# First attention's queries and keys from split inputs, two tiles at a time, and context rows doubled

## The chip, the cores and the metric

The kernel runs on one core of a Trainium2 chip. The metric is the device time of one execution in microseconds (us). The engines of the core are named as in the profile: PE (TensorE, matrix products and transposes), DVE (VectorE), ACT (ScalarE), POOL (GpSimd) and SP, which issues DMAs. Each engine works through its own list of instructions in a fixed order and waits on semaphores.

## What is computed

Two cross-attention blocks follow each other on the same 16 batches. Cut to what matters, with x of 16 x 128 x 256, a context of 16 x 128 x 192 and 16 heads of 16 columns:

```
# block 0
xn, yn = layernorm(x, ln1), layernorm(ctx, ln2)
q = xn @ Wq;  k, v = split(yn @ Wkv)
x = x + softmax(q k^T * 16**-0.5) v @ Wproj + bproj
x = x + gelu(layernorm(x, ln3) @ W1 + b1) @ W2 + b2
# block 1
q = (x * rsqrt(mean(x*x) + 1e-5) * norm_w) @ wq
k, v = split(ctx @ wkv)
q, k = unit(rotate(q)), unit(rotate(k))
x = x + softmax(q k^T * 4) v @ wout
```

## The kernel before

One tile is one batch (128 rows). Three stages run over the 16 tiles, and overlap: the first attention (functions ending in `_a`, with `inputs_a`, `queries_keys_a`, `scores_a`), the MLP over pairs of tiles (`_b`), and the second attention (`_c`). There is no scheduler at run time: every engine's order is written out as a list of calls such as `scores_a(3)`, for PE, DVE, ACT and POOL each, and semaphores hold an engine where a value isn't ready.

A product of two float32 matrices is done in one of two ways. Either `mm` gets float32 operands (the first attention's projections, lines 1068, 1072, 1082 and 1147), or both operands are split into a high and a low part, stored as fp32r, and three matmuls are summed: high by high, high by low, low by high (`HI_LO`, `split_mm`, line 1046, and the MLP, lines 1166 and 1178). The high part is a copy on ACT, the low part is a subtraction on DVE that reads the same data again.

A tile of the first attention goes so. DVE takes statistics, centres and scales x and the context (`statistics`, `centre`, `scale`, lines 2114 to 2140). PE turns both (`inputs_a`), ACT copies the result to SBUF (`inputs_T`, line 547). PE projects queries and keys into `bank_qk` and values into `bank_o`. ACT and DVE split queries and keys (lines 553 and 2146); ACT and POOL multiply them by two masks (lines 559 and 354). PE computes the scores into the four banks `banks_s` (line 1091), DVE reduces them to row maxima (`maxima`, line 2153), splits these (`maxima_split`, 2162 and 2164), PE turns them; then PE computes the same scores again with the maxima taken off (`shifted_a`, 1091 and 1115), ACT takes the exponential (line 575), PE weights the values (1126), turns the result back (`back_a`), DVE divides (`heads_a`, 2170 and 2173), PE turns it (`normed_a`) and projects it (`project_a`, 1147), and DVE adds it to x (`residual_a`, 2179). So every tile needs DVE and PE in turn, and `banks_s` is written twice a tile.

The MLP of a pair begins with `turn_b` on PE, `lnT_b` on ACT and `split_lnT` on DVE (line 2098), behind which the first product `up_b(p, 0)` stands on PE.

`busy(n, bank)` (line 1252) puts n transposes of the identity into a bank that nobody reads. They compute nothing and stand in PE's order in front of waits; there are 98 of them, 35 in front of `up_b(1, 0)`.

## Time and profile before

| what | value |
|---|---|
| median of the runs | 365.31 us (364.48 to 365.33, three runs) |
| the profiled execution, own time | 364.97 us |
| its span, first to last instruction | 363.2 us |
| PE busy | 355.1 us, 98% of the span |
| DVE busy | 278.7 us, 77% |
| ACT busy | 252.7 us, 70% |
| POOL busy | 193.5 us, 53% |
| TensorE's granted clock | 1.00 in every slice |
| DMA share of 16 engines | 0.6, 0.9, 0.6 and 0.4 in the first four fortieths, 0.1 or less after |

PE is busy nearly all the time. DVE's share is an average: it is higher while the first attention runs than later, and the same holds, the other way round, for ACT.

### The profile page before, as it was taken

The numbers are of one execution on the slowest core, as the hardware profiler recorded it, in microseconds if no ns is written. First come the engines' busy times: TensorE is split into PE (matmuls) and PEld (weight loads), VectorE is DVE, ScalarE is ACT, GpSimd is POOL, SyncE is SP. The second block draws the span as 40 slices with busy tenths as digits, with TensorE's granted clock in tenths as the row PEclk, the third lists the DMA queues.
The fourth block names the chain that finished last, engine by engine and source line by source line (L and its number), as shares of the span: only waits on it lengthen the run. The fifth ranks groups of instructions, "written<-read, shape, count | busy, mean of one in ns | idle before, by whom it ended". The sixth has DMA issues, their size and how long they took to land.

```text
span 363.2 us, 11396 instructions
## 1 busy us (share of the span) xinstructions
PE 355.1 (98%) x4492; PEld 322.1 (89%) x4492; DVE 278.7 (77%) x654; ACT 252.7 (70%) x490; POOL 193.5 (53%) x194
## 2 busy tenths in 40 slices
PE   8999999999999998999999999999999999999996
PEld 5988888898788887899999999999999999998885
DVE  3998899868698677767876687787877777868742
ACT  2467766675676674855568988976978679966662
POOL 2357433545735247304687359449465756477920
PEclk9999999999999999999999999999999999999999
DMA  6964110000000000000000000000100000000001
GB/s 181 220 197 130 31 49 28 28 27 27 4 3 2 24 2 2 13 2 14 1 13 13 13 2 7 19 27 11 63 14 13 10 33 27 16 28 16 17 16 43
DMA packets 15724, 12.55 MB, mean 35 GB/s; under 512 B 3252, under 2 KB 15032, under 8 KB 15672
## 3 DMA queue, kind: packets, MB, share of 16 engines
q1 hardware_dynamic: 15664, 11.83, 11.3%
q8 instruction: 36, 0.59, 0.7%
q14 instruction: 16, 0.13, 0.1%
q10 hardware_dynamic: 8, 0.00, 0.0%
HBM read 9.73 MB, written 2.10 MB: 33 GB/s over the span
## 4 chain that ended last, share of the span: by engine, by line
PE 86%; DVE 6%; SPq 3%; issue 2%; DMA 1%; ACT 1%; DVEq 0%; ACTq 0%
PE banks_s L1166 12%; PE bank_qk L1046 10%; PE banks_s L1091 7%; PE bank_o L1178 7%; PE bank_y L1178 6%; PE bank_y L1230 4%; PE banks_s L1219 4%; PE bank_t L1126 4%; PE bank_y L1147 3%; PE bank_t L1046 3%; PE bank_qk L1068 3%; PE bank_o L1082 3%; PE bank_qk L1072 3%; DVE row_max L2153 3%; PE bank_o L1210 2%
## 5 line engine op out<-in xcount | busy, mean ns | idle before, releaser
L400 POOL TENSOR_TENSOR norm_inv<-norm_sq_min,minus_half 128x32 f32<-128x32 f32 x16 | 87.6, 5478 | 47.9 <-DVE norm_sq_min L2248 47.9
L354 POOL TENSOR_TENSOR masked<-qkT_r,halves_t 128x512 fp32r<-128x512 f32 x32 | 32.6, 1040 | 58.5 <-DVE qkT_r L2146 58.5
L2153 DVE TENSOR_REDUCE row_max<-banks_s 128x8 f32<-128x1024 f32 x32 | 37.6, 1216 | 2.9 <-PE banks_s L1091 2.5
L575 ACT ACTIVATE PT<-banks_s 128x1024 f32<-128x1024 f32 x32 | 31.1, 1022 | 10.1 <-PE banks_s L1115 9.7
L1166 PE MATMUL banks_s<-lnT_hi,W_hi 128*128 128x256 f32 x120 | 35.4, 295 | 0.0
L676 ACT ACTIVATE PT<-banks_s 128x1024 f32<-128x1024 f32 x32 | 31.5, 1024 | 5.5 <-PE banks_s L1219 5.2
L1166 PE MATMUL banks_s<-lnT_hi,W_lo 128*128 128x256 f32 x120 | 33.9, 282 | 0.0
L1166 PE MATMUL banks_s<-lnT_lo,W_hi 128*128 128x256 f32 x120 | 33.9, 282 | 0.0
L1091 PE MATMUL banks_s<-masked,qkT_r 32*128 32x256 f32 x768 | 31.5, 294 | 0.9 <-DVE row_max L2153 0.7
L1091 PEld LDWEIGHTS banks_s<-masked,qkT_r 32*128 32x128 f32 x768 | 25.0, 183 | 7.5 <-issue 4.7
L619 ACT ACTIVATE W_s<-banks_s,b_cols 128x256 f32<-128x256 f32 x60 | 25.0, 471 | 6.6 <-PE bank_y L1178 4.7
L2103 DVE TENSOR_TENSOR hT_lo<-W_s,hT_hi 128x512 fp32r<-128x512 f32 x32 | 21.5, 686 | 3.5 <-ACT hT_hi L622 3.4
L1166 PEld LDWEIGHTS banks_s<-lnT_hi,W_hi 128*128 128x128 f32 x120 | 22.8, 190 | 0.6 <-issue 0.6
L1166 PEld LDWEIGHTS banks_s<-lnT_lo,W_hi 128*128 128x128 f32 x120 | 22.9, 191 | 0.0
L1166 PEld LDWEIGHTS banks_s<-lnT_hi,W_lo 128*128 128x128 f32 x120 | 22.8, 190 | 0.0
L378 POOL TENSOR_TENSOR x_all<-x_all,b_row 128x256 f32<-128x256 f32 x16 | 11.5, 741 | 19.0 <-DVE normed L2093 19.0
L559 ACT ACTIVATE masked<-qkT_r,halves_t 128x512 fp32r<-128x512 f32 x32 | 21.3, 717 | 0.2
L2263 DVE SCALAR_TENSOR_TENSOR masked<-bank_o,halves_t,masked 128x256 fp32r<-128x256 f32 x32 | 14.0, 478 | 9.6 <-ACT qkT_r L669 9.5
L622 ACT ACTIVATE hT_hi<-W_s 128x512 fp32r<-128x512 f32 x31 | 19.6, 632 | 1.0
L1178 PE MATMUL bank_o<-W_hi,hT_hi 128*128 128x256 f32 x64 | 19.0, 296 | 0.0
L1178 PE MATMUL bank_y<-W_hi,hT_hi 128*128 128x256 f32 x64 | 18.4, 287 | 0.0
L1178 PE MATMUL bank_y<-W_hi,hT_lo 128*128 128x256 f32 x64 | 18.1, 283 | 0.0
(180 smaller groups left out, 1079.9 us busy)
## 6 DMA issues: line engine op xcount, KB each, us to landing
x_all<-in_x SPq DMA_DIRECT2D x16, 128.0 KB, 2.3
W_s<-in_L_xattn_W SPq DMA_DIRECT2D x2, 1024.0 KB, 7.8
out<-x_all SPq DMA_DIRECT2D x16, 128.0 KB, 1.7
ctx_in<-in_ctx SPq DMA_DIRECT2D x16, 96.0 KB, 3.0
ctx_in<-in_ctx_T SPq DMA_DIRECT2D x16, 64.0 KB, 1.8
ctx_in<-in_ctx_T SPq DMA_DIRECT2D x16, 32.0 KB, 2.1
Wq_s<-in_L_xattn_Wq SPq DMA_DIRECT2D x1, 256.0 KB, 3.7
Wkv_s<-in_L_xattn_Wkv SPq DMA_DIRECT2D x1, 256.0 KB, 3.6
```

Of the source, the lines that this page charges most:

```text
L354: nc.gpsimd.tensor_tensor(masked[:, r, 1, :, half, :], qkT_r[:, r, 1, :, :].bitcast(fp32), ones, ALU.mult)\
L400: nc.gpsimd.tensor_tensor(norm_inv[:, j, :], norm_sq_min[:, j, :], minus_half[:, :], ALU.pow).then_inc(c_norm_inv, 1)
L559: nc.scalar.activation(masked[:, t % RING, 0, :, half, :], qkT_r[:, t % RING, 0, :, :].bitcast(fp32), ACT.Copy, scale=halves_t[:, half:hal ...
L575: nc.scalar.activation(PT[:, 2 * h:2 * h + 2, :], banks_s[:, 2 * h:2 * h + 2, :], ACT.Exp, scale=HD ** -0.5)\
L619: last = nc.scalar.activation(hT[:, m, :], bank[:, 256 * k:256 * k + 256], ACT.Gelu, bias=b1_cols[:, m:m + 1])
L676: nc.scalar.activation(PT[:, 2 * h:2 * h + 2, :], banks_s[:, 2 * h:2 * h + 2, :], ACT.Exp, scale=HD ** 0.5)\
L1046: last = mm(out, a[:, x, k, :], b[:, y, k, :], start=k == n == 0, stop=k == 1 and n == 2)
L1091: last = mm(bank_s[g][:, 2 * TOK * tile:2 * TOK * (tile + 1)], qkT_r[quad(g), r, a, rows + tile, :], masked[quad(g), r, b, columns + tile, ...
L1166: last = mm(bank[:, 256 * (m % 2):256 * (m % 2) + 256], w[:, k, 128 * m:128 * m + 128], act_T[:, k, :], start=k == n == 0, stop=k == KT - ...
L1178: last = mm(bank[:, 0:C1], h[:, m, 128 * j:128 * j + 128], w[:, m, :], start=m == n == 0, stop=m == HM - 1 and n == 2)
L2103: v.tensor_tensor(hT_lo[:, part(u), :], hT[:, part(u), :], hT_hi[:, part(u), :].bitcast(fp32), ALU.subtract).then_inc(b_hT_lo, 1)
L2153: v.tensor_reduce(row_max[:, 8 * h:8 * h + 8], banks_s[:, 2 * h:2 * h + 2, :].rearrange("p n (r k) -> p (n r) k", k=TOK), AX.X, ALU.max).t ...
```

## The change

Five things are changed in the code, and the orders of all engines are written anew.

- The first attention's inputs are split like those of the second: ACT writes the high part into `inT_r`, DVE subtracts the low part (`inputs_lo_a`, new). The weights Wq, Wkv and Wproj are split at the start (three copies on ACT, four subtractions on DVE, new).
- Queries and keys are projected by `queries_a(p)` and `keys_a(p)` for two tiles at once: 12 and 10 matmuls of 256 columns. Both use `bank_qk`, one after the other, so `queries_hi`, `queries_lo`, `keys_hi` and `keys_lo` are four instructions a pair, each of 128 x 512, where `queries_keys_hi` and `queries_keys_lo` were two a tile.
- The projection behind the first attention is a `split_mm` of six matmuls, with `out_lo_a` (new) on DVE.
- The context has 192 columns, 128 and 64. The last 64 are now given twice, so that the second half of the rows is full: the low part of the inputs meets them in one row range and the high part in the other. A product with the context takes five matmuls (`CTX_TERMS`) where a split one took six, in both attentions. The context's normalisation on DVE works on 256 columns where it worked on 192.
- The second attention's weights are loaded into the buffers of the first's, so three waits stand in front of their loads on SP, and `queries_weight`, `context_weight` and `out_weight` wait for the last use of the first attention's splits.

There are now 214 transposes by `busy`, 143 of them in front of `up_b(1, 0)`.

```diff
 HI_LO = ((0, 0), (0, 1), (1, 0))
+CTX_TERMS = ((0, 0, 0), (0, 1, 0), (2, 0, 0), (1, 0, 1), (3, 1, 1))
...
+            def context_mm(out, inputs, columns):
+                for n, (w, a, k) in enumerate(CTX_TERMS):
+                    last = mm(out, inputs[:, a, 2 + k, :], wkv_r[:, w, columns], start=n == 0, stop=n == 4)
+                return last
...
-            def queries_keys_a(t):
...
-                for m in range(KT):
-                    for k in range(KT):
-                        mm(bank_qk[:, 128 * m:128 * m + 128], Wq_s[:, k, 128 * m:128 * m + 128], inT[:, j, k, :],
-                           start=k == 0, stop=k == KT - 1)
...
+            def queries_a(p):
+                if p == 0:
+                    pe.wait_ge(wa_q_lo, 1)
+                pe.wait_ge(a_in_lo, 2 * p + 2)
                 for m in range(KT):
                     for k in range(KT):
+                        for n, (w, a) in enumerate(HI_LO):
+                            last = mm(bank_qk[:, 256 * m:256 * m + 256], wq_r[:, w, k, 128 * m:128 * m + 128],
+                                      inT_r[:, pair_slots(p), a, k, :], start=k == n == 0, stop=k == KT - 1 and n == 2)
+                last.then_inc(a_q_mm, 1)
...
+            def keys_a(p):
...
                 for m in range(KT):
-                    for k in range(2):
-                        last = mm(bank_qk[:, 256 + 128 * m:384 + 128 * m], Wkv_s[:, k, 128 * m:128 * m + 128],
-                                  inT[:, j, 2 + k, :], start=k == 0, stop=k == 1)
+                    for n, (w, a, k) in enumerate(CTX_TERMS):
+                        last = mm(bank_qk[:, 256 * m:256 * m + 256], wkv_r[:, w, 128 * m:128 * m + 128],
+                                  inT_r[:, pair_slots(p), a, 2 + k, :], start=n == 0, stop=n == 4)
+                last.then_inc(a_k_mm, 1)
...
             def values_a(t):
...
-                for k in range(2):
-                    last = mm(bank_o[:, 0:C1], inT[:, t % 2, 2 + k, :], Wkv_s[:, k, C1:], start=k == 0, stop=k == 1)
-                last.then_inc(A["v_mm"], 1)
+                pe.wait_ge(a_in_lo, t + 1)
+                context_mm(bank_o[:, 0:C1], inT_r[:, t % AHEAD], slice(C1, 2 * C1)).then_inc(A["v_mm"], 1)
...
             def project_a(t):
...
-                for k in range(KT):
-                    last = mm(bank_y[:, 0:C1], onT[:, k, :], Wproj_s[:, k, :], start=k == 0, stop=k == KT - 1)
-                last.then_inc(A["proj_mm"], 1)
+                pe.wait_ge(a_onT_lo, t + 1)
+                split_mm(bank_y[:, 0:C1], onT_r[:, :, :, :], wout_r[:, :, :, :]).then_inc(A["proj_mm"], 1)
...
-                split_mm(bank_t[:, C1:2 * C1], inT_r[:, t % 2, :, 2:4, :], wkv_r[:, :, :, C1:]).then_inc(C["v_mm"], 1)
+                context_mm(bank_t[:, C1:2 * C1], inT_r[:, t % 2], slice(C1, 2 * C1)).then_inc(C["v_mm"], 1)
...
-                v.scalar_tensor_tensor(yn[:, j, 0:C2], yn[:, j, 0:C2], rstd[:, j, 1:2], ln2_rows[:, 1, :],
+                v.scalar_tensor_tensor(yn[:, j, :], yn[:, j, :], rstd[:, j, 1:2], ln2_rows[:, 1, :],
                                        ALU.mult, ALU.add).then_inc(A["norm_done"], 1)
...
-            def queries_keys_lo(t):
-                r = t % RING
-                dve.wait_ge(a_qk_hi, t + 1)
-                v.tensor_tensor(qkT_r[:, r, 1, :, :], bank_qk[:, :].rearrange("p (a b) -> p a b", a=4),
-                                qkT_r[:, r, 0, :, :].bitcast(fp32), ALU.subtract).then_inc(a_qk_lo, 1)
+            def inputs_lo_a(t):
+                dve.wait_ge(A["inT_ready"], t + 1)
+                v.tensor_tensor(inT_r[:, t % AHEAD, 1, :, :], bank_t[:, :].rearrange("p (a b) -> p a b", a=4),
+                                inT_r[:, t % AHEAD, 0, :, :].bitcast(fp32), ALU.subtract).then_inc(a_in_lo, 1)
+
+            def queries_lo(p):
+                dve.wait_ge(a_q_hi, p + 1)
+                v.tensor_tensor(qkT_r[:, pair_slots(p), 1, 0:KT, :], pair_bank(bank_qk),
+                                qkT_r[:, pair_slots(p), 0, 0:KT, :].bitcast(fp32), ALU.subtract).then_inc(a_q_lo, 1)
...
+            def out_lo_a(t):
+                dve.wait_ge(A["onT_ready"], t + 1)
+                v.tensor_tensor(onT_r[:, 1, :, :], by_row(bank_y[:, 0:C1]), onT_r[:, 0, :, :].bitcast(fp32), ALU.subtract)\
+                    .then_inc(a_onT_lo, 1)
...
+            act.wait_ge(w_q_loaded, LOADED)
+            nc.scalar.activation(wq_r[:, 0], Wq_s[:, :, :], ACT.Copy).then_inc(wa_q_hi, 1)
+            act.wait_ge(w_att_loaded, LOADED)
+            nc.scalar.activation(wkv_r[:, 0:2, :], Wkv_s[:, :, :], ACT.Copy).then_inc(wa_kv_hi, 1)
             act.wait_ge(rows_spread, 1)
...
-            busy(4, bank_t)
+            busy(8, bank_t)
             inputs_a(0)
-            busy(7, bank_o)
+            busy(15, bank_o)
```

The orders are shown at three places. The first is PE at the start of the program, behind the last warming transposes. Lines 1255 (1291 after) are the fillers of `busy`, 1054 and 1056 (1085 and 1087) turn one tile's inputs, 1068 and 1072 (1097 and 1109) are queries and keys. Before:

```order
L1265 MATMUL banks_s<-ident 128x128 x8
L1255 MATMUL bank_t<-ident 128x128 x4
L1054 MATMUL bank_t<-ident,xn 128x128 x2
L1056 MATMUL bank_t<-ident,yn 128x128 x2
L1255 MATMUL bank_o<-ident 128x128 x7
L1068 MATMUL bank_qk<-inT,Wq_s 128x128 x4
L1072 MATMUL bank_qk<-inT,Wkv_s 128x128 x4
L1054 MATMUL bank_t<-ident,xn 128x128 x2
L1056 MATMUL bank_t<-ident,yn 128x128 x2
```

After:

```order
L1291 MATMUL bank_t<-ident 128x128 x8
L1085 MATMUL bank_t<-ident,xn 128x128 x2
L1087 MATMUL bank_t<-ident,yn 128x128 x2
L1291 MATMUL bank_o<-ident 128x128 x15
L1085 MATMUL bank_t<-ident,xn 128x128 x2
L1087 MATMUL bank_t<-ident,yn 128x128 x2
L1291 MATMUL bank_o<-ident 128x128 x14
L1097 MATMUL bank_qk<-inT_r,wq_r 128x256 x12
L1291 MATMUL bank_o<-ident 128x128 x15
L1109 MATMUL bank_qk<-inT_r,wkv_r 128x256 x10
L1085 MATMUL bank_t<-ident,xn 128x128 x2
```

The queries and keys of tile 0 stood behind 11 fillers and one tile's transposes; they now stand behind those of two tiles, with 37 fillers in front of the queries and 15 more in front of the keys.

The second place is DVE in the first attention: the instructions in front of a reduction to row maxima (`row_max`), that of tile 4 before and of tile 3 after. `xn` and `yn` are the normalised inputs, `on` the divided output of a tile. Before:

```order
L2162 CAST max_cols<-row_max 128x4x4
L2164 TENSOR_TENSOR max_cols<-row_max,max_cols 128x4x4
L2137 SCALAR_TENSOR_TENSOR xn<-xn,rstd,ln_rows 128x256
L2140 SCALAR_TENSOR_TENSOR yn<-yn,rstd,ln_rows 128x192
L2114 BN_STATS stats<-x_all 128x6
L2115 BN_STATS stats<-ctx_in 128x6
L2117 BN_AGGR mean_var<-stats 128x2
L2119 BN_AGGR mean_var<-stats 128x2
L2170 RECIPROCAL row_sums_inv<-bank_o 128x16
L2173 TENSOR_TENSOR on<-bank_o,row_sums_inv 128x256
L2146 TENSOR_TENSOR qkT_r<-bank_qk,qkT_r 128x512
L2153 TENSOR_REDUCE row_max<-banks_s 128x8 x2
```

After:

```order
L2206 TENSOR_TENSOR qkT_r<-bank_qk,qkT_r 128x2x256
L2193 SCALAR_TENSOR_TENSOR xn<-xn,rstd,ln_rows 128x256
L2196 SCALAR_TENSOR_TENSOR yn<-yn,rstd,ln_rows 128x256
L2243 TENSOR_TENSOR onT_r<-bank_y,onT_r 128x256
L2184 SCALAR_TENSOR_TENSOR xn<-x_all,mean_var,ln_rows 128x256
L2186 SCALAR_TENSOR_TENSOR yn<-ctx_in,mean_var,ln_rows 128x256
L2193 SCALAR_TENSOR_TENSOR xn<-xn,rstd,ln_rows 128x256
L2196 SCALAR_TENSOR_TENSOR yn<-yn,rstd,ln_rows 128x256
L2235 RECIPROCAL row_sums_inv<-bank_o 128x16
L2238 TENSOR_TENSOR on<-bank_o,row_sums_inv 128x256
L2211 TENSOR_TENSOR qkT_r<-bank_qk,qkT_r 128x2x256
L2218 TENSOR_REDUCE row_max<-banks_s 128x8 x2
```

Between two reductions there are now low parts of queries (2206), of keys (2211) and of the turned output (2243), and all rows of `yn` are 256 wide.

The third place is PE in front of the first up product of the second pair (`W_hi` by `lnT_hi` into `banks_s`, line 1166 before and 1200 after; behind `...` in the piece of before stand the rest of 24 down products of the first pair, in that of after 17 more down products and a group of 12 up products of the first pair). Before:

```order
L1133 MATMUL bank_o<-ident,oT 128x128 x4
L1046 MATMUL bank_qk<-wkv_r,inT_r 128x256 x6
L1155 MATMUL bank_t<-ident,normed 128x128 x4
L1147 MATMUL bank_y<-Wproj_s,onT 128x256 x2
L1178 MATMUL bank_o<-W_hi,hT_hi 128x256
L1178 MATMUL bank_o<-W_lo,hT_hi 128x256
...
L1178 MATMUL bank_o<-W_hi,hT_lo 128x256
L1166 MATMUL banks_s<-lnT_hi,W_hi 128x256
```

After:

```order
L1189 MATMUL bank_t<-ident,normed 128x128 x4
L1127 MATMUL banks_s<-masked,qkT_r 128x256 x24
L1151 MATMUL banks_s<-maxT,picks_wide 128x128 x16
L1139 MATMUL bank_qk<-ident,max_cols 128x128
L1175 MATMUL bank_y<-ident,on 128x128 x2
L1212 MATMUL bank_o<-W_hi,hT_hi 128x256
...
L1078 MATMUL bank_qk<-wkv_r,inT_r 128x256 x5
L1072 MATMUL bank_y<-wout_r,onT_r 128x256 x6
L1200 MATMUL banks_s<-lnT_hi,W_hi 128x256
```

Behind the transposes of the pair (`normed`) now stand the shifted scores of tile 14 (1127, 1151) and the turning of tile 15's maxima (1139). The shifted scores of tile 15, `weighted_a` and `back_a` of tiles 14 and 15, `normed_a(14)`, `project_a(14)` and six down products are behind the up product now; before, they stood in front of it.

## Rows read from the trace of the kernel before

**Rows 1.** Busy time in three stretches: span, then us and count for each engine.
```profile
20.64:160.92 140.28, 137.28 (x2118) 119.86 (x2117) 117.45 (x270) 95.54 (x168) 65.36 (x88) 1.00 0.11 33
20.64:63.85 43.21, 42.41 (x677) 37.20 (x679) 40.24 (x98) 28.70 (x49) 19.87 (x27) 1.00 0.26 80
160.92:363.20 202.28, 198.80 (x2266) 186.71 (x2264) 147.29 (x343) 148.61 (x308) 120.74 (x86) 1.00 0.06 19
```

**Rows 2.** Timeline of PE in the first attention: start us, length us, group.
```profile
70.31 1.07 PE L1126 MATMUL bank_t<-PT,vals 128*17 128x128 f32 x32
71.31 0.98 PE L1091 MATMUL banks_s<-masked,qkT_r 32*128 32x256 f32 x24
72.12 0.56 PE L1115 MATMUL banks_s<-maxT,picks_wide 32*128 32x128 f32 x16
...
73.10 1.06 PE L1068 MATMUL bank_qk<-inT,Wq_s 128*128 128x128 f32 x8
74.00 1.06 PE L1072 MATMUL bank_qk<-inT,Wkv_s 128*128 128x128 f32 x8
74.89 0.60 PE L1133 MATMUL bank_o<-ident,oT 128*128 128x128 f32 x4
...
81.37 1.03 PE L1082 MATMUL bank_o<-Wkv_s,inT 128*128 128x256 f32 x4
82.24 1.03 PE L1147 MATMUL bank_y<-Wproj_s,onT 128*128 128x256 f32 x4
```

**Rows 3.** The chain in order of time: start us, length us, engine, tile, line.
```profile
186.96 1.42 PE banks_s L1166 x12
188.38 1.43 PE bank_qk L1046 x12
```

**Rows 4.** Timeline of PE: filler transposes and the matmuls behind them.
```profile
25.41 1.25 PE L1255 MATMUL bank_y<-ident 128*128 128x128 f32 x10
26.59 0.99 PE L1091 MATMUL banks_s<-masked,qkT_r 32*128 32x256 f32 x24
```

**Rows 5.** Timeline of DVE: one of each kind of its instructions.
```profile
42.63 0.41 DVE L2179 TENSOR_TENSOR x_all<-x_all,bank_y 128x256 f32<-128x256 f32 x1
...
43.25 0.48 DVE L2137 SCALAR_TENSOR_TENSOR xn<-xn,rstd,ln_rows 128x256 f32<-128x256 f32 x1
43.65 0.41 DVE L2140 SCALAR_TENSOR_TENSOR yn<-yn,rstd,ln_rows 128x192 f32<-128x192 f32 x1
43.98 0.42 DVE L2114 BATCH_NORM_STATS2 stats<-x_all 128x6 f32<-128x256 f32 x1
...
45.51 0.26 DVE L2170 RECIPROCAL row_sums_inv<-bank_o 128x16 f32<-128x16 f32 x1 [0.64 <-PE bank_o L1133]
...
46.15 0.68 DVE L2146 TENSOR_TENSOR qkT_r<-bank_qk,qkT_r 128x512 fp32r<-128x512 f32 x1
46.74 2.34 DVE L2153 TENSOR_REDUCE row_max<-banks_s 128x8 f32<-128x1024 f32 x2
```

**Rows 6.** Timeline of POOL, ACT and PE at the start of the program.
```profile
11.91 0.60 ACT L547 ACTIVATE inT<-bank_t 128x512 f32<-128x512 f32 x1 [2.84 <-PE bank_t L1056]
16.74 2.04 POOL L354 TENSOR_TENSOR masked<-qkT_r,halves_t 128x512 fp32r<-128x512 f32 x2 [2.32 <-DVE qkT_r L2146]
18.98 0.98 PE L1091 MATMUL banks_s<-masked,qkT_r 32*128 32x256 f32 x24
```

**Rows 7.** Timeline of DVE: the first reduction, and the second pair's `lnT_lo`.
```profile
20.64 2.34 DVE L2153 TENSOR_REDUCE row_max<-banks_s 128x8 f32<-128x1024 f32 x2
...
160.24 0.68 DVE L2098 TENSOR_TENSOR lnT_lo<-bank_t,lnT_hi 128x512 fp32r<-128x512 f32 x1
```

**Rows 8.** Timeline of PE: the first up product of the second pair.
```profile
161.98 0.28 PE L1166 MATMUL banks_s<-lnT_hi,W_hi 128*128 128x256 f32 x1
```

**Rows 9.** Timeline of POOL and DVE: a mask product beside a split of maxima.
```profile
98.49 2.04 POOL L354 TENSOR_TENSOR masked<-qkT_r,halves_t 128x512 fp32r<-128x512 f32 x2 [1.69 <-DVE qkT_r L2146]
98.52 1.04 DVE L2164 TENSOR_TENSOR max_cols<-row_max,max_cols 128x16 f32<-128x16 f32 x1
```

1952 lines of the change are left out of this document (1013 added, 939 removed).

## The prediction

> **What bounds the kernel now.** I read the busy table first: PE works in 98% of the span, DVE in 77%, so the first guess is that whatever is taken off PE is gained. Then the chain of waits in order of time, which runs from one PE group straight to the next [rows 3]: it shows that PE's work, not a wait, sets the time over most of the span. Then busy time in stretches, because a share over the whole span hides which stage is near a second limit. From the first reduction of row maxima to the end of the second pair's low part, which is nearly the whole first attention, PE is busy 137.28 of 140.28 us and DVE 117.45; behind it DVE is busy 147.29 of 202.28 [rows 1]. The stretch inside it from 20.64 to 63.85 is the one to look at: PE 42.41 and DVE 40.24 of 43.21 us [rows 1]. There both engines are nearly full. So the first attention has little room on DVE, and this is where the change adds DVE work.
>
> **What PE loses and gains.** Prices are from one start to the next. Queries and keys of a tile take 0.90 + 0.89 us, its values 0.87 [rows 2], and its projection is the same two 128x256 float32 products, 0.87. A group of twelve split matmuls of 256 columns takes 1.42 [rows 3], 0.119 each. The new queries and keys are 22 of these a pair, 11 a tile, 1.31 us where 1.79 stood: 0.48 less. Values are five, 0.60: 0.27 less. The projection is six, 0.71: 0.15 less. Over 16 tiles that is 7.7 + 4.4 + 2.4. The second attention has two matmuls fewer a tile, 32 x 0.119 = 3.8. Removed: 18.2 us. Added: 116 filler transposes. Ten of them stand between 25.41 and 26.59 [rows 4], 0.118 each: 13.7 us. If nothing else moved, PE would be 4.5 us shorter: 365.0 - 4.5 = 360.5. The fillers stand in front of waits, so part of them covers waiting that would be there anyway; they can't be counted as a loss by themselves.
>
> **What DVE gains, and the sum.** I take DVE's list from the first reduction (`maxima(0)`) to `split_lnT(1)`, 117.45 us busy before [rows 1, 7], and go through what is added and what is moved out of it.
> - Twelve `inputs_lo_a`, 128x512 with one operand in PSUM, like `qkT_r` at 46.15, which gives way to the next after 0.59 [rows 5]: 0.60 each, 7.2.
> - Fourteen `out_lo_a`, 128x256 with one operand in PSUM, like the residual at 42.63, 0.33: 4.7.
> - One low part of Wproj: 0.6.
> - 22 instructions on `yn` that go from 192 to 256 columns: 0.40 for 256 (43.25 to 43.65) and 0.33 for 192 (43.65 to 43.98) [rows 5]: 22 x 0.07 = 1.5.
> - Queries' and keys' low parts are fourteen of 128x512 in either kernel: nothing. ACT has the same trade.
> - Out of the stretch go two `scale` (0.73 each), one `statistics` (0.9: 43.98 to 45.51 less the 0.64 of waiting), two `heads_a` (0.64), two `residual_a` (0.33), one `split_hT` (0.6), one memset (0.3) [rows 5]: 5.2 in all.
>
> Net 8.8, so DVE has 126.3 us to do in there.
>
> When does it begin? The first scores stood at 18.98 and the reduction at 20.64 [rows 6, 7]. Now tile 0's turned inputs are copied from 11.91 on for 0.60 [rows 6] and subtracted for 0.60; tile 1's transposes reuse the bank, so the same follows once more; twelve matmuls 1.4, copy and subtraction 1.2, ten matmuls 1.2, copy and subtraction 1.2, then POOL's masks 2.04 [rows 6]. DVE's own list in between (normalisation of four tiles, the weights' low parts at 1.2) is longer than this chain at two places: I come to 24.9 for the first scores and 26.2 for the reduction, 5.6 later than before. Half of what PE spends on fillers lies here, and it costs nothing, for the queue behind it can't start.
>
> Then the first up product of the second pair can start at 26.2 + 126.3 + 0.1 = 152.6 if DVE never idles, where it stood at 161.98 [rows 8], about 1 us behind its operand. Behind it PE had 363.2 - 162.0 = 201.2 us. Moved behind it are the shifted scores of tile 15 (0.81 + 0.5), two `weighted_a` (2.0), two `back_a` (1.0) [rows 2], `normed_a(14)`, one more projection and six down products (1.5 together); eight fillers more, 0.9; 31 context matmuls less, 3.7. Net 3.0. The sum is 152.6 + 201.2 + 3.0 = 356.8, and 1.8 outside the span (365.0 - 363.2): 358.6.
>
> What is missing is DVE's idle time in the stretch. Lower bound nothing: 358.6, which PE's own 360.5 overrules. Upper bound: the share in the stretch where both engines are nearly full, 40.24 of 43.21 [rows 1], 6.9% idle: 126.3 / 0.931 is 9.4 more, 368.0. There each engine waits for the other in turn. In the changed kernel PE has more room beside DVE than there, since its work without fillers shrinks by 0.9 us a tile while DVE's grows, so more values should lie ready when DVE comes to them; but PE's order is fixed and `banks_s` still goes back and forth twice a tile. I take half the share, 4.5 us: **363.1**. That is 1.9 below the profiled execution; the median of the runs shown is 0.3 above that execution, which I leave to the range.
>
> ACT and POOL. ACT gets four copies of weights and loses nothing; at 95.54 of 140.28 us [rows 1] it has room, except at the start, where the copies of Wq and Wkv stand in front of the rows that DVE's `centre(0)` needs. Bounds: 0, if the weights land before those rows are ready, to 2.0 for both copies (by the 0.60 of 128x512); in the range. SP now waits for the first weights' low parts in front of the second's loads, and the inputs of tile 9 on stand behind it on SP; DVE asks for them over ten calls later, so 0 to 3 us, taken as 0. The wider context rows are 128 KB a tile where 96 were: hidden after the first tiles.
>
> A rule to weigh: DVE's group at 42.63 to 46.74 shows an instruction starting about 0.08 us before the recorded end of the one in front (46.15 + 0.68 is 46.83, the next starts at 46.74) [rows 5]. The Trainium skill, VectorE: DVE Perf Modes, section The DRAIN you can't avoid, says that the next operation doesn't start until the pipe is empty. Priced by whole recorded lengths the 26 new subtractions would come to 2 us more, 365 in all; the trace does not agree that the full length is paid, and the sum goes by starts.
>
> **The rivals.**
> - PE alone sets the time, and DVE keeps up: 360.5. For it: 98% against 77%. Against it: 40.24 of 43.21 us with the smaller load.
> - DVE sets the pace of the first attention at 6.9% idle: 368.0, slower than before. Its place is the loop of scores, maxima, turned maxima and exponentials on `banks_s`, its price 9.4 us, and it decides from 6.4 us of DVE idle time on, 4.8% of the stretch (358.6 + 6.4 = 365.0). Each further hold-up adds to it: a split of maxima that meets a mask product on POOL takes 1.04 us [rows 9], so another order can move several microseconds. The Trainium skill, SBUF — State Buffer, section SBUF: two separate sides, says that a DVE operation with two SBUF inputs and a GpSimd operation hold a shared port pair for their whole length; the trace agrees, as the split at 98.52 ends at 99.56 and POOL's first of two products, 2.04 together from 98.49 on, near 99.5. Sixteen splits that each meet one would add 14 us by that rule.
> - The start goes wrong: the weights' copies on ACT hold `centre(0)` up, or the fillers are longer than the waits they cover. 2 to 3 us on top of 363.1: about 366.
>
> **Chances.** The forecast 0.42 (its own range 361 to 366), PE alone 0.22, DVE's pace 0.28, the start 0.08. A change under 0.3%, 1.1 us, can't be told from none here: faster is below 364.2, slower above 366.4. Faster: 0.22 + 0.25 of the forecast = 0.47. Within: 0.13 + 0.04 + 0.02 = 0.19. Slower: 0.04 + 0.24 + 0.06 = 0.34. The range 358.5 to 369.5 leaves one in ten on either side.
>
> **What would show it.** Right: PE's busy share falls while its idle time in the first attention grows, waits of PE on DVE's subtractions and splits appear, and DVE is busy over 93% between its first reduction and the second pair's `lnT_lo`; that product starts near 157; the first reduction is near 26; behind it PE is as full as now. Wrong: DVE idle over 6.4 us in there, a first reduction later than 28, or PE waiting on ACT or POOL. If the up product starts at 153 and PE is full, PE alone was the case.

## The result and the profile after

The changed kernel takes 368.00 us (median of ten, 365.88 to 368.45), the one before 364.91 (median of ten, 364.48 to 365.33): ratio 1.0064, 95% interval 1.0047 to 1.0082. It is 3.1 us slower; I had forecast 1.9 faster. Its ten times stand in two groups, four near 366 and six near 368; the profiled execution took 368.45, with a span of 366.3 us, so it is one of the second group.

The page of the changed kernel, busy time and the chain's shares by engine (the chain is the work that ended last, followed back from the last instruction); the last line is the same share in the kernel before:

```profile
PE 355.1 (97%) x4544; PEld 323.1 (88%) x4544; DVE 294.2 (80%) x681; ACT 259.0 (71%) x498; POOL 195.6 (53%) x194
...
PE 72%; DVE 13%; POOL 5%; issue 4%; ACT 3%; POOLq 1%; DVEq 0%; ACTq 0%
...
PE 86%; DVE 6%; SPq 3%; issue 2%; DMA 1%; ACT 1%; DVEq 0%; ACTq 0%
```

PE's busy time did not fall at all. DVE's rose by 15.5 us over the whole span, and the chain leaves PE for other engines more often.

Where the time went is seen best from two marks that both kernels have, the first and the last of DVE's sixteen pairs of reductions of row maxima. In the timeline of DVE of the changed kernel they stand here, with the second pair's `lnT_lo` (the counterparts before are in [rows 7]):

```profile
27.91 2.34 DVE L2218 TENSOR_REDUCE row_max<-banks_s 128x8 f32<-128x1024 f32 x2
...
147.26 2.35 DVE L2218 TENSOR_REDUCE row_max<-banks_s 128x8 f32<-128x1024 f32 x2 [1.39 <-PE banks_s L1127]
...
159.22 0.69 DVE L2154 TENSOR_TENSOR lnT_lo<-bank_t,lnT_hi 128x512 fp32r<-128x512 f32 x1 [0.28 <-ACT lnT_hi L614]
```

The last reduction of the kernel before, same view:

```profile
140.13 2.36 DVE L2153 TENSOR_REDUCE row_max<-banks_s 128x8 f32<-128x1024 f32 x2 [1.70 <-PE banks_s L1091]
```

So there are three parts, in us of the two profiled spans (363.2 and 366.3):

| | before | after | difference |
|---|---|---|---|
| start, to the first reduction | 20.64 | 27.91 | +7.27 |
| body, first to last reduction | 119.49 | 119.35 | -0.14 |
| behind, last reduction to the end | 223.07 | 219.04 | -4.03 |

The start loses 7.3 us, what stands behind gains 4.0, and the body, where the change was to free PE, gains nothing. Busy time in the body, before (first fence) and after, with the same columns as [rows 1]; the fourth row of the second fence is the stretch that answers to the first row of [rows 1]:

```profile
20.64:140.13 119.49, 116.56 (x1839) 101.06 (x1841) 100.55 (x228) 80.51 (x141) 59.25 (x79) 1.00 0.13 37
```

```profile
27.91:60.00 32.09, 30.45 (x476) 26.94 (x478) 31.41 (x69) 21.28 (x39) 17.08 (x23) 1.00 0.26 76
60.00:90.00 30.00, 28.95 (x492) 25.89 (x485) 28.85 (x72) 18.55 (x33) 12.74 (x19) 1.00 0.10 29
90.00:159.91 69.91, 67.55 (x1062) 60.08 (x1060) 62.96 (x138) 52.53 (x93) 35.18 (x45) 1.00 0.03 8
27.91:159.91 132.00, 126.95 (x2019) 112.90 (x2017) 123.23 (x276) 92.35 (x164) 65.00 (x85) 1.00 0.10 29
27.91:147.26 119.35, 114.71 (x1870) 101.73 (x1869) 111.59 (x250) 81.37 (x143) 63.37 (x82) 1.00 0.10 31
159.91:366.30 206.39, 202.72 (x2362) 188.66 (x2360) 150.00 (x351) 156.68 (x319) 120.73 (x86) 1.00 0.07 20
```

In the body DVE goes from 100.55 to 111.59 us and PE from 116.56 to 114.71. From 27.91 to 90 DVE works 60.3 of 62.1 us: it is full there. Its idle time stands behind that, 7.0 us between 90 and 159.91, and the longest waits in it are for PE: 2.4 us for score matmuls (the last reduction above waited 1.39) and 1.1 for projections. The second pair's up product starts 0.84 us behind the start of `lnT_lo`, 0.15 behind its end:

```profile
160.06 0.36 PE L1200 MATMUL banks_s<-lnT_hi,W_hi 128*128 128x256 f32 x1
```

It stood at 161.98 [rows 8] and I had put it at 152.6 plus 4.5, 157.1. PE's timeline in the body shows the new products, where [rows 2] had the float32 ones:

```profile
69.62 0.84 PE L1078 MATMUL bank_o<-wkv_r,inT_r 128*128 128x256 f32 x5
70.31 0.82 PE L1291 MATMUL bank_qk<-ident 128*128 128x128 f32 x6
...
78.03 0.98 PE L1072 MATMUL bank_y<-wout_r,onT_r 128*128 128x256 f32 x6
78.85 0.60 PE L1169 MATMUL bank_o<-ident,oT 128*128 128x128 f32 x4
```

From start to the next start, five matmuls of the values take 0.69 here, where I had priced 0.60, and six of the projection 0.82, where I had priced 0.71. The twelve of the queries and the ten of the keys cost more too, 1.53 and 1.29 where I had 1.42 and 1.19:

```profile
62.20 1.60 PE L1097 MATMUL bank_qk<-inT_r,wq_r 128*128 128x256 f32 x12
63.73 0.98 PE L1127 MATMUL banks_s<-masked,qkT_r 32*128 32x256 f32 x24
...
66.03 1.45 PE L1109 MATMUL bank_qk<-inT_r,wkv_r 128*128 128x256 f32 x10
67.32 0.38 PE L1175 MATMUL bank_y<-ident,on 128*128 128x128 f32 x2
```

Each group that stands between other products takes about 0.1 us more than the price from the groups of twelve of [rows 3], behind which a group of the same kind follows. And PE waits more: it is idle for 4.6 us of the body, where it was for 2.9. PE's three largest waits there, us in total, times, longest:

```profile
PE banks_s L1127 <- DVE row_max L2218: 1.8, 4, 1.0
PE bank_qk L1139 <- DVE max_cols L2229: 0.8, 1, 0.8
PE banks_s L1127 <- POOL masked L358: 0.8, 2, 0.6
```

The chain in order of time shows the same from another side. A piece of it in the changed kernel:

```profile
53.97 1.21 DVE row_max L2218
55.19 0.33 DVE x_all L2249
55.51 0.25 DVE max_cols L2227
...
55.79 0.67 DVE max_cols L2229
56.45 0.34 DVE stats L2170
56.79 0.26 DVE stats L2171
...
57.18 0.95 DVE row_max L2218
...
58.30 1.22 DVE row_max L2218
...
59.57 0.98 PE banks_s L1127 x23
```

Before, the chain ran from one PE group to the next as in [rows 3] over most of the first attention too. A piece of it:

```profile
34.78 0.39 PE banks_s L1115 x15
35.17 1.09 PE bank_qk L1068 x8
36.26 0.89 PE bank_qk L1072 x8
```

### The profile page after: what moved, and what is told of

It reads as the page before. It is cut to its first block, busy times and chain, and to the rows that moved or that the text cites. A ratio compares the mean times of both kernels' runs of the same rounds, so it can differ in the third digit from the quotient of the medians.

```text
span 366.3 us, 11549 instructions
## 1 busy us (share of the span) xinstructions
PE 355.1 (97%) x4544; PEld 323.1 (88%) x4544; DVE 294.2 (80%) x681; ACT 259.0 (71%) x498; POOL 195.6 (53%) x194
## 4 chain that ended last, share of the span: by engine, by line
PE 72%; DVE 13%; POOL 5%; issue 4%; ACT 3%; POOLq 1%; DVEq 0%; ACTq 0%
PE banks_s L1200 11%; PE bank_o L1212 7%; PE bank_y L1212 6%; PE banks_s L1127 5%; PE bank_qk L1072 5%; DVE row_max L2218 4%; PE bank_y L1266 4%; PE bank_t L1162 3%; POOL norm_inv L404 3%; PE banks_s L1255 3%; PE bank_y L1072 3%; PE bank_t L1078 2%; PE bank_qk L1097 2%; PE bank_qk L1078 2%; PE bank_qk L1109 2%
## 5 line engine op out<-in xcount | busy, mean ns | idle before, releaser
L358 POOL TENSOR_TENSOR masked<-qkT_r,halves_t 128x512 fp32r<-128x512 f32 x32 | 33.0, 1054 | 15.2 <-issue 14.1
L397 POOL TENSOR_TENSOR inT_r<-ctx_in,inT_r 128x256 fp32r<-128x256 f32 x16 | 11.8, 737 | 24.5 <-ACT inT_r L668 24.5
L339 POOL TENSOR_TENSOR var_eps<-mean_var,eps_t 128x2 f32<-128x2 f32 x16 | 4.1, 256 | 37.2 <-DVE mean_var L2175 37.2
## 6 DMA issues: line engine op xcount, KB each, us to landing
x_all<-in_x SPq DMA_DIRECT2D x16, 128.0 KB, 2.6
ctx_in<-in_ctx SPq DMA_DIRECT2D x16, 128.0 KB, 2.8
ctx_in<-in_ctx_T SPq DMA_DIRECT2D x16, 128.0 KB, 2.2
out<-x_all SPq DMA_DIRECT2D x16, 128.0 KB, 1.8
```

Source lines behind the costliest of these rows:

```text
L358: nc.gpsimd.tensor_tensor(masked[:, r, 1, :, half, :], qkT_r[:, t % AHEAD, 1, :, :].bitcast(fp32), ones, ALU.mult)\
```

## The experiments

All times are medians, and gains and losses are differences of medians. "Body" and "behind" are the parts of the table above, read off each kernel's profiled execution.

**The second attention's five matmuls, alone and taken back.** The kernel before with one matmul of six left out of the second attention's products on the context:

```
-                split_mm(bank_qk[:, C1:], inT_r[:, t % 2, :, 2:4, :], wkv_r[:, :, :, 0:C1])
+                context_mm(bank_qk[:, C1:], inT_r[:, t % 2, :, 2:4, :], wkv_r[:, :, :, 0:C1])
...
+            def context_mm(out, a, b):
+                for n, (x, y, k) in enumerate(((0, 0, 0), (0, 1, 0), (1, 0, 0), (0, 0, 1), (0, 1, 1))):
+                    last = mm(out, a[:, x, k, :], b[:, y, k, :], start=n == 0, stop=n == 4)
```

> The kernel before with one part of the change alone: the second attention's keys and values take five matmuls instead of six (the product of the low part of the last 64 context rows is left out, which doubled rows would have given). 32 matmuls of 256 columns less on PE. If PE's list sets the time to the end: 32 x 0.119 = 3.8 us gained, 361.1. If the last 37 us are set by POOL's four inverse norms (5.4 us each, in a chain with DVE), only the 26 of them ahead of the last down product count: 3.1 us gained at most, and the distance from the end of that product to the end of the kernel stays 37 us. If the saving meets waits elsewhere too: under 2 us.

Measured: 361.37 us, ratio 0.9894 (0.9872 to 0.9916), 3.65 less than the kernel before beside it (365.02). Start 20.43, body 119.56, behind 219.61 (223.07 before). The saving arrives. The distance from the last down product's last matmul to the end of the span is 37.4 us before (325.78 to 363.2) and 37.2 here (322.41 to 359.6), so nearly all of it was won ahead of it.

The same thing done whole, with the rows loaded twice and the weights laid out for it:

```
+                sp.dma_start(ctx_in[C2B:, j, TOK:2 * TOK], ctx_T[t, 128:C2, :]).then_inc(c_loaded[j], LOADED)
...
+                        v.tensor_copy(by_tile(wkv_r[0:C2B, 1, k, 0:C1]), keys[0:C2B]).then_inc(wc_lo, 1)
+                        v.tensor_tensor(by_tile(wkv_r[C2B:, 0, k, 0:C1]), keys[C2B:], by_tile(wkv_r[C2B:, 0, k, 0:C1]).bitcast(fp32),
+                                        ALU.subtract).then_inc(wc_lo, 1)
```

> The kernel before with the second attention's part of the change done whole: its context rows 128 to 191 are loaded twice, their weights are laid out as the changed kernel has them, and keys and values take five matmuls each. Nothing is left out. Against the kernel without that product (361.4) it adds one transfer of 32 KB a tile on SP and two short copies of weights on DVE. Theory PE's list: 361 to 362. Theory that the transfers or DVE's copies come in the way: above 363.

Measured: 361.40 us, ratio 0.9898 (0.9884 to 0.9912). This is the version to take: 3.6 us faster than the kernel before and 6.6 faster than the changed one.

The changed kernel with a sixth matmul back in each of these products:

```
-                context_mm(bank_qk[:, C1:], inT_r[:, t % 2], slice(0, C1))
+                context_mm(bank_qk[:, C1:], inT_r[:, t % 2], slice(0, C1), CTX_TERMS + ((2, 1, 0),))
```

> The changed kernel with a sixth matmul (low part by low part of the first 128 rows) back in each of the second attention's products on the context, 32 matmuls of 256 columns. Theory that its saving there is whole and the loss lies in the first attention's part: 3.5 to 4 us slower, 371.7. Theory that the saving is swallowed in the changed kernel (waits behind 160 us, the tail on POOL): under 2 us slower.

Measured: 371.06 us, 3.1 more than the changed kernel; start 27.84, body 119.22, behind 222.04. So the saving is there in the changed kernel as well, and without it the rest of the change, the first attention's part and the new orders together, would cost 371.06 - 364.91 = 6.2 us.

**DVE's load.** More of it in the kernel before:

```
+                wait(dve, spare_done, t)
+                v.tensor_reduce(spare[:, :], bank_qk[:, :].rearrange("p (n k) -> p n k", n=8), AX.X, ALU.max).then_inc(spare_done, 1)
                 v.tensor_tensor(qkT_r[:, r, 1, :, :], bank_qk[:, :].rearrange("p (a b) -> p a b", a=4),
```

> The kernel before with 16 more DVE instructions in the first attention: a reduction of one 128x512 bank, about 0.6 us, ahead of each tile's low part of queries and keys; its result is used by nobody. DVE gets 14 x 0.6 = 8.4 us more in the stretch from the first reduction to the second pair's low part, as much as the change adds. PE's list is untouched. DVE's busy share there would go from 84% to 90%. Theory DVE (load itself is the price): 3 to 8 us slower, 368 to 373. Theory order (the changed kernel's loss is from its start, its order and what it moves behind, not from load): under 2 us slower.

Measured: 371.89 us, ratio 1.0183 (1.0163 to 1.0203), 6.9 more. The sixteen instructions took 10.9 us, and the body grew by 6.2 for 8.9 us more of DVE's work in it:

```profile
22.05:147.72 125.67, 117.48 (x1837) 100.94 (x1841) 109.43 (x243) 80.18 (x140) 59.69 (x79) 1.00 0.11 33
```

DVE works 109.43 of 125.67 us there, 87%, and still each us of it cost over half a us. A share of busy time of 87% is no sign of room when the order is fixed. The added instruction stands right in front of the low part for which POOL's masks and the scores wait, so the run does not tell the load itself from its place; added work at a place with slack was not tried.

Less of it in the changed kernel:

```
+                n = TOK if t < AHEAD else 8
+                v.tensor_tensor(inT_r[:, t % AHEAD, 1, :, 0:n], bank_t[:, :].rearrange("p (a b) -> p a b", a=4)[:, :, 0:n],
...
+                n = TOK if t == 0 else 16
+                v.tensor_tensor(onT_r[:, 1, :, 0:n], by_row(bank_y[:, 0:C1])[:, :, 0:n], onT_r[:, 0, :, 0:n].bitcast(fp32), ALU.subtract)\
```

> The changed kernel with DVE's new subtractions cut to a small corner of each tile: inputs' low parts from tile 4 on write 8 of 128 columns a piece, the attention output's low parts from tile 1 on 16 of 128. The rest of the low parts is left over from earlier tiles, so that part of the computation is left out. PE's and all other lists are as they were. DVE has about 12 x 0.50 + 15 x 0.25 = 9.7 us less to do in the first attention. Theory DVE: 5 to 9 us gained, the kernel near 360. Theory PE: under 1.5 us gained, only at places where PE waits on DVE for a moment.

Measured: 366.67 us, 1.3 less than the changed kernel. In the body of the profiled execution, DVE's busy time falls by 6.7 us, the body by 1.4:

```profile
27.81:145.76 117.95, 114.39 (x1870) 101.68 (x1869) 104.92 (x249) 81.28 (x143) 63.53 (x82) 1.00 0.11 31
```

That is as little as the theory of PE's list allowed: DVE's load alone does not set the changed kernel's pace.

**PE's load.** Less of it in the changed kernel, then DVE and PE light together:

```
+                for n, (w, a, k) in enumerate(CTX_TERMS[0:3]):
+                    last = mm(bank_o[:, 0:C1], inT_r[:, t % AHEAD, a, 2 + k, :], wkv_r[:, w, C1:], start=n == 0, stop=n == 2)
...
+                for n, (x, y) in enumerate(HI_LO):
+                    last = mm(bank_y[:, 0:C1], onT_r[:, x, 0, :], wout_r[:, y, 0, :], start=n == 0, stop=n == 2)
```

> The changed kernel with 80 matmuls of 256 columns less on PE in the first attention: values take three of five and the projection three of six (the second half of the contraction is left out). DVE's, ACT's and POOL's lists and all fillers are as they were. PE has 80 x 0.119 = 9.5 us less. Theory PE (PE's list with its fillers sets the first attention): 6 to 9.5 us gained, about 360. Theory coupled (PE and DVE wait for each other in turn, relieving one alone gains little, as 9.7 us less on DVE gained 1.3): under 3 us gained, or a loss where the clock falls.

> The changed kernel with both loads lightened in the first attention: DVE by 9.7 us (low parts cut to a corner) and PE by 9.5 us (three matmuls for values, three for the projection). Theory PE: 1 to 2 us below the kernel with PE light alone. Theory coupled: 6 to 10 us gained against the changed kernel, several times the sum of the two single gains.

Measured: 364.95 us with PE light, 364.22 with both. The times of the first stand in groups too, six from 363.6 to 364.3 and three from 365.8 to 366.2 at the same granted clock, and its median falls between them. Group against group (365.9 and 368.1 in the changed kernel) PE light is worth 2.0 us, not the 3.05 of the medians, which is inside what the coupled theory allowed; both together are worth 3.8 by the lowest group (362.2 against 365.9) as by the medians. The two bodies:

```profile
27.36:145.26 117.90, 108.87 (x1804) 94.27 (x1804) 110.68 (x249) 80.29 (x142) 63.37 (x82) 1.00 0.10 31
```

```profile
26.98:143.19 116.21, 107.80 (x1804) 94.11 (x1804) 104.11 (x249) 80.20 (x142) 63.11 (x82) 1.00 0.10 32
```

With PE down to 107.80 and DVE to 104.11, neither is full, and the body is only 3.1 us shorter. Both single theories fall, and so does the part of the coupled one that said relieving both would give several times the sum: 3.8 against 1.3 + 2.0. What is left, by exclusion and not shown by a run of its own, is handing over between engines in an order that was written for other loads. Over this body the second largest entry of the chain by line is "issue" (time for which the profile shows no wait), 16.5%, where it was 7.1% in the changed kernel's.

PE's load less in the kernel before:

```
-                for k in range(KT):
-                    last = mm(bank_y[:, 0:C1], onT[:, k, :], Wproj_s[:, k, :], start=k == 0, stop=k == KT - 1)
+                last = mm(bank_y[:, 0:C1], onT[:, 0, :], Wproj_s[:, 0, :], start=True, stop=True)
```

> The kernel before with less for PE in the first attention: values and projection take one float32 matmul of two (half of each contraction is left out), 32 x 0.43 = 13.8 us less on PE; nothing else changes. Theory PE was the bound of the first attention before: 9 us or more gained, so that a faster product has to pay off where DVE does not take it back. Theory coupled (PE and DVE wait for each other in turn there already, as 9.6 us more on DVE cost 6.9): 3 to 7 us gained.

Measured: 360.00 us, ratio 0.9877 (0.9861 to 0.9892), 4.8 less for 13.8 us of PE work by the price from starts (PE's busy time fell by 11.2), as the coupled theory said. Body 116.01, behind 221.65. A us taken off PE in the first attention was worth 0.35 us in the kernel before, a us put on DVE in front of its low parts cost 6.9 / 10.9 = 0.63.

**The score banks.** A theory that I formed on the way: the four score banks are held in turn by scores, maxima, shifted scores and exponentials, and that ring sets the pace. Exponentials over half of their columns, in the changed kernel, in the one before, and in the changed one with PE light; and maxima over half of theirs:

```
+                n = 512 if t < 2 else 256
+                nc.scalar.activation(PT[:, 2 * h:2 * h + 2, 0:n], banks_s[:, 2 * h:2 * h + 2, 0:n], ACT.Exp, scale=HD ** -0.5)\
```

```
-                                    banks_s[:, 2 * h:2 * h + 2, :].rearrange("p n (r k) -> p (n r) k", k=TOK),
+                                    banks_s[:, 2 * h:2 * h + 2, :].rearrange("p n (r k) -> p (n r) k", k=TOK)[:, :, 0:TOK if t < 2 else TOK // 2],
```

> The changed kernel with ACT's exponentials of the first attention over half of their columns from tile 2 on (the other half is left over from earlier tiles). Each shortens the time in which the score banks are held by about 0.43 us, 0.86 a tile, 12.0 over 14 tiles; no other instruction changes, and ACT had room before (92 of 131 us). Theory loop (the four score banks, held by scores, maxima, shifted scores and exponentials in turn, some 7.0 us a tile of a period of 8.0, set the first attention): 6 to 12 us gained, 356 to 362. Theory PE or coupled orders: under 3 us gained.

> The kernel before with the same shorter exponentials. Theory that PE's own list bounds it and the loop of the score banks doesn't: under 2 us gained, 363 to 365. Theory that the loop was the limit already: 6 us or more gained, below 359.

> The changed kernel with the shorter exponentials and with PE light (three matmuls for values and for the projection). Theory loop: little below the kernel with the shorter exponentials alone, or as much below it as PE light gained by itself (3 us). Theory PE and loop in turn: more than the sum of the two.

> The changed kernel with DVE's reductions of row maxima over half of their columns from tile 2 on (the maxima of the first 64 keys only). Each tile's pair of reductions holds the score banks about 1.07 us less, and DVE has as much less to do, 14.9 us in all. Theory loop: 8 to 14 us gained. Theory that neither the loop nor DVE sets the pace: under 3 us, as with the 9.7 us that were taken off DVE outside the loop (1.3 gained).

Measured: exponentials 369.06 after (body 120.06), 364.96 before (ratio 1.0010, 0.9998 to 1.0021), 365.82 with PE light; maxima 365.10, 2.9 less than the changed kernel for 9.7 us less on DVE in the body:

```profile
27.41:143.69 116.28, 114.41 (x1870) 101.83 (x1869) 101.91 (x249) 81.31 (x143) 64.33 (x82) 1.00 0.11 32
```

In the body ACT's busy time fell by 8.7 us in the changed kernel (81.37 to 72.70) and by 10.7 in the one before, and nothing was gained in either, nor on top of PE light, so the hold of the banks by the exponentials is not the limit.

The profiled execution with the shorter exponentials, 366.40, shows something else. Up to its first reduction its program is the changed kernel's own, and the reduction comes 2.57 us earlier:

```profile
25.34 2.35 DVE L2219 TENSOR_REDUCE row_max<-banks_s 128x8 f32<-128x1024 f32 x2
```

Its span is 2.0 us shorter than the 366.3 above (364.3), with a body 0.7 longer and 218.90 behind. That is the distance of the two groups of the changed kernel's times, so these are most likely executions with a start of 25.3 and of 27.9 us; an execution of the changed kernel itself from the shorter group has no trace.

**The fillers.** The changed kernel without the 68 fillers of the body, and without the 66 behind the last down product:

```
             pe.wait_ge(a_maxT, 1)
-            busy(8, bank_y)
             pe.wait_ge(a_maxed, 4)
             shifted_a(0)
-            busy(12, bank_y)
```

> The changed kernel without the 68 filler transposes that stand between the first scores and the projection of tile 3 (33 to 88 us in its trace). Theory PE (PE's list with its fillers is the limit of the first attention): 68 x 0.118 = 8.0 us less on PE, of which most is gained, the second up product of the MLP (160.06 us now) near 153 and the kernel near 361. Theory DVE (DVE and the loop of scores, maxima and exponentials set the pace, fillers stand where PE would wait anyway): the product within 1 us of 160, the kernel within 1 us of 366 to 368. If the granted clock falls because PE pauses, the kernel gets slower and the clock row shows it.

> The changed kernel without the 66 fillers behind the last down product of the MLP (from 334 us on). Theory POOL tail (the last 37 us are a chain of POOL's inverse norms, 5.4 us each, and DVE): the starts of POOL's last three inverse norms don't move and the kernel stays within 1 us of 368 (366 in its quicker executions), unless the granted clock falls at the end. Theory PE: up to 66 x 0.118 = 7.8 us gained.

Measured: 369.94 us without the first, 1.9 more than the changed kernel. The granted clock of the first stretch falls to 0.84, where it was 1.00, and a group of 24 score matmuls (0.98 us at the higher level) and one of 32 (1.07) get longer:

```profile
27.55:60.00 32.45, 28.08 (x414) 24.05 (x413) 29.07 (x66) 19.20 (x34) 14.44 (x19) 0.84 0.24 74
```

```profile
38.05 1.65 PE L1127 MATMUL banks_s<-masked,qkT_r 32*128 32x256 f32 x24 [0.44 <-POOL masked L358]
...
40.04 1.91 PE L1162 MATMUL bank_t<-PT,vals 128*17 128x128 f32 x32
```

Behind these waits, from 37.55 to 47.55, the granted clock is 0.52, the level of 1.2 GHz. The fillers of the body cover waits, and keep the clock up; their 8.0 us on PE cost nothing that shows. Without those of the tail the kernel takes 367.39, 0.6 less for 7.8 us of PE work: nearly all of them are cover.

**The tail.** The version with doubled rows, POOL's last three inverse norms over half of their columns:

```
+                n = 2 * H if t < 13 else H
+                nc.gpsimd.tensor_tensor(norm_inv[:, j, 0:n], norm_sq_min[:, j, 0:n], minus_half[:, 0:n], ALU.pow).then_inc(c_norm_inv, 1)
```

> The kernel with doubled rows in the second attention alone (361.4), and POOL's inverse norms of the last three tiles over 16 of 32 columns (the keys' norms are left over from earlier tiles): about 2.7 us less each, which shows whether POOL's chain sets the last 37 us. Theory POOL tail: 5 to 8 us gained, 354 to 356, where PE's own work in the tail takes over. Theory PE tail: under 1 us.

Measured: 361.21 us against 361.40. POOL's three instructions take 2.90 us in place of 5.43, and what is won on POOL is lost behind it: the distance from the last one's end to the end of the span grows from 16.3 us (344.7 to 361.0, in an execution of 362.76) to 19.0 (340.6 to 359.6, in one of 361.39):

```profile
337.69 2.90 POOL L403 TENSOR_TENSOR norm_inv<-norm_sq_min,minus_half 128x16 f32<-128x16 f32 x1 [2.12 <-DVE norm_sq_min L2263]
```

My theory of a tail set by POOL falls. PE's list with its fillers may be as long as POOL's chain there, which would explain why taking away either gives next to nothing; taking both away at once was not tried.

**The start.** First the kernel before with 60 more fillers ahead of its first product:

```
-            busy(7, bank_o)
+            busy(67, bank_o)
```

> The kernel before with 60 more fillers ahead of the first queries and keys, so that the first reduction comes near 27.5 us instead of 20.64, as late as in the changed kernel; all else is as before. Theory start (the changed kernel loses what its first pair takes longer, whatever DVE does meanwhile): 5 to 7 us slower, 370 to 372. Theory that DVE's work done meanwhile makes up for it: under 3 us slower.

Measured: 371.08 us, ratio 1.0159 (1.0134 to 1.0184), 6.3 more. The profiled execution was a shorter one, 368.83, and shows the link: first reduction 24.46, 3.8 later than in [rows 7], body 119.55, behind 222.99, and a span of 367.0, 3.8 more than 363.2. A plain shift passes on whole. Three of the five times are 2.2 to 2.7 us longer than this one; no trace shows where.

Then the changed kernel with a shorter way to its first scores (second bank for tile 1's inputs and for the first pair's keys, the first pair's parts drawn forward):

```
+            return bank_y if t == 1 else bank_t
...
+            return bank_o if p == 0 else bank_qk
...
             inputs_lo_a(0)
-            statistics(2)
-            centre(2)
             inputs_lo_a(1)
             weights_kv_lo()
+            statistics(2)
+            centre(2)
             queries_lo(0)
```

> The changed kernel with a shorter way to its first scores: tile 1's inputs are turned into a bank of their own, so they need not wait for tile 0's low part; the first pair's keys go to another bank than its queries and follow them at once; DVE, ACT and POOL do the first pair's parts ahead of the normalisation of tiles 3 and 4. No instruction is left out or added but for 17 fillers less. First scores expected near 22.5 us (26.44 now), first reduction near 23 to 24 (27.91 now). The late start on the kernel before moved its end by as much as the first reduction (3.8 for 3.8 us in the profiled execution). Theory start (1 for 1): 363.5 to 365. Theory DVE (it is busy from 14 us on, so that what is drawn forward only pushes other work back): within 1.5 us of 368, or slower.

> As the kernel with the shorter start, and the second tile's scores and maxima follow the first tile's at once, ahead of the inputs of tiles 3 and 4. Theory start: as low as that one or up to 2 us below. Theory DVE: the inputs of the second pair come later by what is drawn forward, and the kernel is within 1.5 us of 368.

Measured: 373.41 and 373.42 us, 5.4 more than the changed kernel. The first reduction came at 24.49 and 24.48, 3.4 earlier, and the body grew to 128.3 and 128.0. Busy time of the second, then the wait of PE that stands in it, and DVE's behind it:

```profile
24.48:50.00 25.52, 19.57 (x257) 17.36 (x256) 21.17 (x48) 9.72 (x19) 10.32 (x15) 0.87 0.15 42
```

```profile
32.67 0.66 PE L1094 MATMUL bank_t<-ident,xn 128*128 128x128 f32 x2 [4.24 <-DVE yn L2204]
...
33.41 2.91 PE L1106 MATMUL bank_qk<-inT_r,wq_r 128*128 128x256 f32 x12
...
36.99 0.69 DVE L2214 TENSOR_TENSOR qkT_r<-bank_qk,qkT_r 128x512 fp32r<-128x512 f32 x1 [2.70 <-ACT qkT_r L577]
```

The second pair's inputs came later by what I had drawn forward on DVE, PE stood idle for 4.24 us, and the twelve matmuls behind took 2.91 us, where the same group takes 1.68 in the changed kernel at 28.46. Then DVE idled in its turn, 4.4 of these 25.5 us. So an earlier first reduction is worth nothing when the second pair's inputs come later for it. These two orders let the engines wait for each other and the clock fall, and the runs do not tell how much of the loss is due to each. They don't speak against the start either: the shift of 3.8 and the execution above whose start is 2.57 us shorter both passed a change of the start on, whole and to about four fifths. How much of the 7.3 us an order with PE kept busy could win back is left open.

## Why the prediction was wrong

The forecast was 358.6 plus 4.5; its terms against the profiled execution of 368.45:

| term | forecast | measured | |
|---|---|---|---|
| first reduction | 26.2 | 27.91 | +1.7 |
| DVE's work from there to the end of `split_lnT(1)` | 126.3 | 123.2 | -3.1 |
| DVE's idle time in it | 4.5 | 8.8 | +4.3 |
| from its end to the up product | 0.1 | 0.15 | 0.0 |
| behind the up product | 204.2 | 206.2 | +2.0 |
| outside the span | 1.8 | 2.15 | +0.4 |

**The step that failed** is "I take half the share, 4.5 us", with its reason that "PE has more room beside DVE" so that "more values should lie ready when DVE comes to them". DVE was idle for 6.7% of the stretch (8.8 of 132.0), nearly the 6.9% of my upper bound and not half of it. That it met the bound's number is chance, as its place is another: in the part up to 90 us, where both engines are nearly full as in the stretch of [rows 1] that gave the bound, DVE idled only 1.8 of 62.1 us; the other 7.0 stand behind it, 10% of 69.9 us, and 2.4 and 1.1 of them are waits for PE's scores and projections. So the room on PE did not become values lying ready. Less of it was there than I had priced, and PE's fixed order kept DVE waiting for products that stood late in its list. Which place of that order costs how much, no run shows.

**The start** was put 1.7 us too short for the profiled execution: DVE had 20.93 us of work ahead of the first reduction, where it had 13.91 before. I counted a chain with DVE's list "longer than this chain at two places"; from 14.2 us on DVE's list ran with one wait of 0.27 us. In the execution with the first reduction at 25.34 the same term would have been 0.9 too long, so my 26.2 lies between the two. The step above fails in either: from the first reduction to the up product I had 130.9 us, and it took 132.2 in the profiled execution and 132.7 in that one (158.05 less 25.34). Busy time of the start, before and after:

```profile
0.00:20.64 20.64, 19.00 (x113) 15.53 (x113) 13.91 (x44) 8.55 (x15) 7.42 (x20) 1.00 0.79 203
```

```profile
0.00:27.91 27.91, 25.42 (x167) 21.58 (x168) 20.93 (x56) 9.98 (x16) 9.90 (x24) 1.00 0.74 209
```

**What PE gains** was mis-sized too. Values and projection should be 0.69 and 0.82 by the rows above: (0.09 + 0.11) x 16 = 3.2 us more. Queries and keys add (0.11 + 0.10) x 8 = 1.7. Of the 18.2 us removed 13.3 are left, and 13.7 came back as fillers, so PE's own list is as long as before; its busy time is 355.1 in both kernels. A tile's products shrink by 0.6 us, not by the 0.9 on which "more room beside DVE" rested, and the rival "PE alone, 360.5" never had its 4.5 us.

**Behind the up product** the five-matmul products gave what I said: 3.7 forecast, 3.65 and 3.1 measured by the two runs. The rest took 2.0 more than forecast. It is not waiting: PE idled 3.7 of 206.4 us there (last row of the busy times in the section on the result), and 3.5 of 202.3 before [rows 1]. So the work that I had counted as moved or new behind it was put too low; which part of it was not traced.

**The rivals.** The number of "DVE's pace", 368.0, is the measured median, but its mechanism stands only in part. Its point of decision (6.4 us of idle time) was passed, and the chain does run more through DVE. Yet 6.7 us less on DVE in the body gave 1.4, and shorter exponentials in the ring that it named gave nothing. The total, too, is made up otherwise: its 9.4 us of idle time were 8.8, DVE's work 3.1 less, the start 1.7 and the rest 2.0 more. The runs show several limits within 2 to 4 us of each other: DVE light 1.3, PE light 2.0, both 3.8, maxima 2.9. Of the third rival, the start, the first half was worth 0.5 us: the copies of the weights on ACT put `centre(0)` at 9.64 where it stood at 9.11. The second half, fillers longer than the waits that they cover, was worth about as much in the profiled execution: PE turned the first inputs at 11.88, and they were ready at 11.31. The signs that I had named came out against the forecast: idle DVE over 6.4 us, PE waiting for POOL too (0.8 us for masks in the body), the up product at 160. DVE was busy 93.3% in the stretch, just above the 93% that I had called right; my own 4.5 us would have made it 96.6%, so this sign did not tell the cases apart.

**Summed up by runs:** the second attention's part of the change is worth 3.1 to 3.65 us; the rest costs 6.2. In the kernel before, DVE time cost 0.63 us a us and freed PE time gave 0.35. With 11.0 us more on DVE in the body and 1.9 less on PE that would be some 6 us slower (an estimate from these two prices); the body stayed equal, so the new order seems to have won that back, and the 7.3 us of the start (4.7 in the executions with the shorter one) were lost. That a shift of the start passes on is shown, by the 3.8 for 3.8 and by the 2.0 for 2.57. That an order can win it back without losing it again in the body is not: the two runs that tried it lost more.

## What to carry to other kernels

Where two engines are each over 85% busy in a written order, price work by a run in which it is added to the old kernel: here a us added on DVE at 84%, in front of a value that others wait for, cost 0.63, and a us freed on PE gave 0.35, so trading PE time for DVE time one to one would lose. Take the price of a group of matmuls from a group with the same neighbours. Split a change by stage and try each part alone; the half in a stage with one clear limit held all of the gain, and the other half cost nearly twice as much. And cut the span at marks that both kernels have (first and last of a repeated instruction), since that shows start, body and rest at once, where the whole-span busy shares hardly moved.
